# Three step buffers used in turn in a masked attention kernel: comparisons three units ahead, masks two

## The reference

```python
h = einsum('bnf,hfo->bhno', x, W)
s1 = einsum('bhno,ho->bhn', h, a1)
s2 = einsum('bhno,ho->bhn', h, a2)
e = leaky_relu(s1[..., :, None] + s2[..., None, :], negative_slope=0.2)
attn = softmax(where(adj > 0, e, NEG_INF), axis=-1)
h_prime = einsum('bhnm,bhmo->bhno', attn, h)
out = layernorm(x + transpose_and_reshape(h_prime), axis=-1)
```

## Time and profile before

| | |
|---|---|
| three runs, us | 2890.48, 2895.20, 2897.44 |
| the profiled execution | 2894.5 us, span 2892.8 us, mean granted TensorE clock 0.977 |
| one batch, start to start | 352 to 354 us; 32 units 284 to 287, the start of the next 66 to 69 |
| busy, share of the span | TensorE 92%, weight load 80%, VectorE 88%, ScalarE 81%, GpSimd 37% |
| ScalarE's comparisons (L603) | 3440, 2099.4 us busy |
| DMA | 390.20 MB, mean 135 GB/s |
| the chain that ended last | TensorE 33%, ScalarE 29%, VectorE 18%, issue 14%, DMA 3%, GpSimd 2% |

### The profile page before, as it was taken

The page is one execution under the profiler, slowest core; times in us unless marked ns, Lnnn a source line. Parts: engine busy times, 40 slices in busy tenths (PEclk is TensorE's granted clock), DMA queues, the critical chain, the costliest instruction groups (busy, mean ns, idle before and its releaser), DMA issues.

```text
span 2892.8 us, 126180 instructions
## 1 busy us (share of the span) xinstructions
PE 2666.2 (92%) x52546; PEld 2311.9 (80%) x52546; DVE 2532.7 (88%) x3881; ACT 2338.9 (81%) x3894; POOL 1083.5 (37%) x1011
## 2 busy tenths in 40 slices
PE   6999989999899998999989989899998999989996
PEld 3698867989579994898949988499884998759996
DVE  6898978999799997899888998889888998889996
ACT  4599965999569994799938998399983999839994
POOL 4633335333353324433253332533326333163331
PEclk9999999999999999999999999999999999999998
DMA  6467642675527754377543775447644476345763
GB/s 176 118 132 174 148 132 78 143 174 142 137 65 167 169 139 114 75 174 166 135 102 81 174 166 129 105 103 173 163 119 114 108 171 157 106 117 121 172 159 97
DMA packets 281205, 390.20 MB, mean 135 GB/s; under 512 B 161856, under 2 KB 161856, under 8 KB 280672
## 3 DMA queue, kind: packets, MB, share of 16 engines
q1 hardware_dynamic: 253536, 315.24, 40.7%
q0 software_dynamic: 27136, 67.12, 14.2%
HBM read 313.52 MB, written 34.14 MB: 120 GB/s over the span
## 4 chain that ended last, share of the span: by engine, by line
PE 33%; ACT 29%; DVE 18%; issue 14%; DMA 3%; POOL 2%; DVEq 1%; ACTq 0%; SPq 0%; POOLq 0%
ACT m_pos L603 26%; PE ps L526 12%; PE ps L497 6%; PE ps L557 6%; PE ps L558 5%; DVE m_neg L837 3%; DMA y<-in_x 3%; ACT adj_cut L569 2%; DVE m_pos L830 2%; DVE prod L801 2%; DVE prod_d L804 1%; DVE m_pos L816 1%; ACT xT L575 1%; PE ps L433 1%; DVE b_both L799 1%
## 5 line engine op out<-in xcount | busy, mean ns | idle before, releaser
L603 ACT ACTIVATE m_pos<-ps,s_steep 128x512 fp8e4<-128x512 f32 x3440 | 2099.4, 1087 | 371.3 <-PE ps L447 295.4
L526 PE MATMUL ps<-b_both,m_pos 128*128 128x130 f16 x16384 | 1018.8, 221 | 81.7 <-DVE total L666 63.0
L558 PE MATMUL ps<-d_lo,m_neg 128*128 128x65 f16 x16384 | 1034.7, 194 | 16.7 <-issue 16.4
L557 PE MATMUL ps<-d_hi,m_neg 128*128 128x65 f16 x16384 | 1034.9, 193 | 7.7 <-issue 7.6
L526 PEld LDWEIGHTS ps<-b_both,m_pos 128*128 128x128 fp8e5 x16384 | 965.7, 98 | 93.4 <-issue 91.4
L557 PEld LDWEIGHTS ps<-d_hi,m_neg 128*128 128x128 fp8e5 x16384 | 1016.0, 98 | 28.6 <-issue 28.5
L558 PEld LDWEIGHTS ps<-d_lo,m_neg 128*128 128x128 fp8e5 x16384 | 1006.7, 97 | 24.4 <-issue 10.3
L830 DVE TENSOR_TENSOR m_pos<-m_pos,maskT 128x1024 uint32<-128x1024 uint32 x512 | 630.4, 1249 | 165.6 <-ACT m_pos L603 153.3
L1000 POOL TENSOR_TENSOR den_scaled<-den_inv,bound 128x4 f32<-128x4 f32 x256 | 257.5, 1006 | 1269.1 <-DVE den_inv L677 1207.8
L837 DVE TENSOR_TENSOR m_neg<-m_pos,maskT 128x2048 uint32<-128x2048 uint32 x256 | 583.9, 2281 | 0.3
L497 PE MATMUL ps<-W_sb,xT 128*128 128x512 f32 x1024 | 461.4, 612 | 65.7 <-DVE prod_d L804 63.9
(11 more groups left out here) (95 smaller groups left out, 1578.5 us busy)
## 6 DMA issues: line engine op xcount, KB each, us to landing
adj_in<-in_adj SPq DMA_DIRECT2D x266, 512.0 KB, 4.7
s_bc<-s_rows SPq DMA_DIRECT2D x258, 256.0 KB, 3.6
x_in<-in_x SPq DMA_DIRECT2D x134, 256.0 KB, 4.2
x_sum<-in_x POOLq DMA_DIRECT2D x128, 256.0 KB, 4.9
y<-in_x POOLq DMA_DIRECT2D x32, 1024.0 KB, 9.9
out<-y SPq DMA_DIRECT2D x32, 1024.0 KB, 7.1
maskT<-adj_cut SPq DMA_TRANSPOSE x264, 3.6
m_neg<-in_x SPq DMA_DIRECT2D x10, 256.0 KB, 3.1
```

What stands on the lines that cost most here:

```text
L526: mm = pe.matmul(acc, mask, b_both[:, j, h, :, :], start=(j == 0 and it % 2 == 0), stop=(j == JC - 1 and it % 2 == 1))
L557: pe.matmul(acc, mask, d_hi[:, j, h, :], start=(j == 0), stop=False)
L558: mm = pe.matmul(acc, mask, d_lo[:, j, h, :], start=False, stop=(j == JC - 1))
L603: ins = nc.scalar.activation(chunk(m_pos[h % 2], j, 0, BLK), ps[:, BANK_S1 + h % 2, :], ACT.Relu, bias=s2_steep[:, j, h:h + 1], scale=STEE ...
```

## The change

There are three `m_pos` buffers instead of two, used in turn by the number of the unit in its batch. `before(unit)` gives how many units back the last user of the same buffer is (3; over the seam of two batches 2, 2 and 5 for units 0, 1 and 2).

- ScalarE's comparisons of unit u now wait for `neg_made` and `pos_summed` of u-3. Its program keeps the order; `copy_s1` moves from unit 30 behind the comparisons of unit 31.
- TensorE spreads the row of u+3 between the second and third tile of the negative sums of u, after a wait for ScalarE's comparisons of u+1; before, it spread u+2 between positive and negative sums. The row of unit 2 is spread at chunk 8 of the batch start.
- VectorE's iteration of u: `make_neg(u+1)`, maxima of x, `take_pos(u)`, scores, layer norm, two `make_pos` of u+2, comparisons of u+3, `take_neg(u)`. In the batch start the comparisons of unit 2 stand where `make_neg(1)` stood. In unit 31: `take_pos(31)`, masks of the next unit 0, `take_neg(31)`.
- `dve_slots` counts from u-3; the number of comparisons of each engine in a batch stays the same.
- SyncE loads the s1 row of u+3 instead of u+2.
- TensorE starts unit 0 when 7 chunks and a half are split, waits again before the second half and before its last three chunks, and turns the x tile of unit 0 behind the positive sums instead of ahead of them.

```diff
@@ -81,6 +81,6 @@
-        k, h = divmod((unit - 2) % UNITS, H)
-        if unit in (0, 1) or k * H + h == STAT_UNIT:
+        k, h = divmod((unit - 3) % UNITS, H)
+        if unit in (0, 1, 2) or k * H + h == STAT_UNIT:
             return DVE_SLOTS[1]
-        if (k and h in (2, 3)) or k * H + h in (0, STAT_UNIT + 1):
+        if k and h in (2, 3):
             return DVE_SLOTS[2]
@@ -88,2 +88,6 @@
+    def before(unit):
+        return {0: UNITS - (UNITS - 2), 1: UNITS + 1 - (UNITS - 1), 2: UNITS + 2 - (UNITS - 3)}.get(unit, 3)
     FIRST = 6
@@ -135,3 +139,3 @@
-        m_pos = [sb(f"m_pos{i}", [P, JC // 2, 2 * BLK], FP8) for i in range(2)]
+        m_pos = [sb(f"m_pos{i}", [P, JC // 2, 2 * BLK], FP8) for i in range(3)]
         m_neg = [sb(f"m_neg{i}", [P, JC // 2, 2 * BLK], FP8) for i in range(2)]
...
@@ -377,5 +381,10 @@
                                 store_block(g - 1, 1)
-                        if unit == UNITS - 2:
+                        if unit == UNITS - 3:
                             sp.wait_ge(s1_stored, 16 * KB * (b + 2))
-                        load_s1(u + 2, h % 2)
+                        if unit == UNITS - 1:
+                            sp.sem_inc(waited[sp.engine], 1)
+                            with sp.If(b < B - 1):
+                                load_s1(u + 3, (h + 1) % 2)
+                        elif unit:
+                            load_s1(u + 3, (h + 1) % 2)
                         for t in range(JC):
@@ -393,2 +402,6 @@
                                 load_x(JC * (b + 1) + t, t % 2, ((b + 1) * (JC // 2) + t // 2) % (NBLK * IT // 2))
+                        if unit == 0:
+                            with sp.If(b < 1):
+                                load_s1(2, 0)
+                            load_s1(u + 3, (h + 1) % 2)
                         if unit == STURN_UNIT + 1:
@@ -444,3 +457,7 @@
-            def spread_s1(unit):
+            def spread_s1(unit, u):
+                if type(u) is not int:
+                    pe.wait_ge(step_act, at(step_act, QUADS * (u - 1)))
+                    pe.sem_inc(waited[pe.engine], 1)
...
@@ -489,2 +506,4 @@
                         pe.wait_ge(s1_T_copied, b + 1)
+                    if jc == 8:
+                        spread_s1(2, b * UNITS + 2)
                     if jc == 1:
@@ -506,7 +525,6 @@
                         if unit == 0:
-                            pe.wait_ge(hi_d_made, b * JC + JC - 1)
-                            turn_x(JC * (b + 1), x_in[0][:], x_loaded[0], b * (JC // 2), 0)
                             pe.wait_ge(tiny_made, b + 1)
-                            pe.wait_ge(lo_made, at(lo_made, 2 * JC * (b + 1) - 2))
+                            pe.wait_ge(lo_made, at(lo_made, 2 * JC * b + JC - 1))
+                            pe.sem_inc(waited[pe.engine], 1)
                         pe.wait_ge(pos_read, at(pos_read, u))
@@ -517,2 +535,5 @@
                             pe.sem_inc(waited[pe.engine], 1)
+                            if unit == 0 and qd:
+                                pe.wait_ge(lo_made, at(lo_made, 2 * JC * (b + 1) - 7))
+                                pe.sem_inc(waited[pe.engine], 1)
                             for it in range(IT):
@@ -520,6 +541,6 @@
                                 for j in range(qd * JQ, (qd + 1) * JQ):
-                                    if unit == 0 and it == 0 and j == JC - 1:
-                                        pe.wait_ge(lo_made, at(lo_made, 2 * JC * (b + 1) - 1))
+                                    if unit == 0 and it == 0 and j >= JC - 3:
+                                        pe.wait_ge(lo_made, at(lo_made, 2 * JC * b + 2 * j + 1))
                                         pe.sem_inc(waited[pe.engine], 1)
-                                    mask = chunk(m_pos[hp], j, it * P, P).bitcast(FP8_WIDE)
+                                    mask = chunk(m_pos[unit % 3], j, it * P, P).bitcast(FP8_WIDE)
@@ -532,9 +553,5 @@
                             pe.wait_ge(lo_made, at(lo_made, 2 * JC * (b + 1)))
-                        if unit == UNITS - 2:
-                            pe.wait_ge(s1_T_copied, b + 2)
-                        spread_s1((unit + 2) % UNITS)
                         if unit == STAT_UNIT + 1:
                             turn_s1(b + 1)
-                        if unit and unit in TILE_UNIT:
+                        if unit in TILE_UNIT:
                             t = TILE_UNIT.index(unit)
@@ -553,2 +570,9 @@
                         for it in range(IT):
+                            if it == IT // 2 and unit < UNITS - 3:
+                                spread_s1(unit + 3, u + 3)
+                            if it == IT // 2 and unit >= UNITS - 2:
+                                if unit == UNITS - 2:
+                                    pe.wait_ge(s1_T_copied, b + 2)
+                                spread_s1(unit + 2 - UNITS, u + 2)
                             acc = ps[:, 2 + hp, it * O1:(it + 1) * O1]
@@ -590,3 +614,4 @@
-            def compare(u, h, unit):
+            def compare(u, unit):
+                h = unit % H
                 act.wait_ge(s1_spread, u + 1)
@@ -594,5 +619,5 @@
-                act.wait_ge(neg_made, at(neg_made, u - 1))
+                act.wait_ge(neg_made, at(neg_made, u - before(unit) + 1))
                 act.sem_inc(waited[act.engine], 1)
-                act.wait_ge(pos_summed, at(pos_summed, u - 1))
+                act.wait_ge(pos_summed, at(pos_summed, u - before(unit) + 1))
                 act.sem_inc(waited[act.engine], 1)
@@ -602,3 +627,3 @@
                             j = qd * JQ + c
-                            ins = nc.scalar.activation(chunk(m_pos[h % 2], j, 0, BLK), ps[:, BANK_S1 + h % 2, :], ACT.Relu,
+                            ins = nc.scalar.activation(chunk(m_pos[unit % 3], j, 0, BLK), ps[:, BANK_S1 + unit % 2, :], ACT.Relu,
                                                        bias=s2_steep[:, j, h:h + 1], scale=STEEP, saturate=False)
@@ -621,3 +646,3 @@
             act.wait_ge(s2_turned, 1)
-            compare(0, 0, 0)
+            compare(0, 0)
@@ -637,7 +662,6 @@
                             copy_scores(b + 1)
-                        if unit == STAT_UNIT + 2:
-                            copy_s1(b + 1)
                         if unit < UNITS - 1:
-                            compare(u + 1, (h + 1) % H, unit + 1)
+                            compare(u + 1, unit + 1)
                         else:
+                            copy_s1(b + 1)
                             exponentials(b + 1)
@@ -646,3 +670,3 @@
                                 act.sem_inc(waited[act.engine], 1)
-                                compare(u + 1, 0, 0)
+                                compare(u + 1, 0)
                         for i in late:
@@ -805,6 +829,8 @@
-            def compare(u, h, nth, unit):
+            def compare(u, unit, nth):
+                h = unit % H
                 hp = h % 2
-                dve.wait_ge(neg_made, at(neg_made, u - 1))
+                dve.wait_ge(neg_made, at(neg_made, u - before(unit) + 1))
                 dve.sem_inc(waited[dve.engine], 1)
@@ -815,3 +841,3 @@
                         j = qd * JQ + c
-                        ins = V.tensor_scalar(chunk(m_pos[hp], j, 0, BLK).bitcast(FP8_WIDE), s1_bc[hp][:], s2_neg[:, j, h:h + 1],
+                        ins = V.tensor_scalar(chunk(m_pos[unit % 3], j, 0, BLK).bitcast(FP8_WIDE), s1_bc[hp][:], s2_neg[:, j, h:h + 1],
                                               STEP_UP, ALU.is_gt, ALU.mult, saturate=False)
@@ -819,8 +845,8 @@
-            def make_pos(u, h, mask, qd, first_of_block=None):
-                hp = h % 2
+            def make_pos(u, unit, qd, blk):
+                mask = maskT[unit // H % 2]
                 if qd == 0:
-                    if first_of_block is not None:
+                    if unit % H == 0:
                         for slot in range(2):
-                            dve.wait_ge(piece_turned[slot], at(piece_turned[slot], 16 * IT * (first_of_block + 1)))
+                            dve.wait_ge(piece_turned[slot], at(piece_turned[slot], 16 * IT * (blk + 1)))
                             dve.sem_inc(waited[dve.engine], 1)
@@ -829,20 +855,12 @@
                 js = slice(qd * JQ // 2, (qd + 1) * JQ // 2)
-                V.tensor_tensor(words(m_pos[hp][:, js, :]), words(m_pos[hp][:, js, :]),
+                V.tensor_tensor(words(m_pos[unit % 3][:, js, :]), words(m_pos[unit % 3][:, js, :]),
                                 words(mask[:, js, :]), ALU.bitwise_and).then_inc(pos_made, 1)
-            def make_neg(u, h, mask):
-                hp = h % 2
+            def make_neg(u, unit):
+                mask = maskT[unit // H % 2]
                 dve.wait_ge(unit_done, at(unit_done, u - 1))
                 dve.wait_ge(pos_made, at(pos_made, QUADS * (u + 1)))
-                V.tensor_tensor(words(m_neg[hp][:]), words(m_pos[hp][:]), words(mask[:]), ALU.bitwise_xor
```

(47 more changed lines are left out.)

14 lines of the change are left out of this document (7 added, 7 removed).

## The result

| | before | after |
|---|---|---|
| median of 15 runs each, taken in turn | 2895.3 us | 2912.5 us |
| lowest to highest | 2890.2 to 2901.9 | 2902.3 to 2923.1 |
| profiled execution, its span | 2894.5, 2892.8 | 2903.2, 2901.4 |

The ratio is 1.0059, 95% interval 1.0045 to 1.0073: slower by 0.6%, where the prediction said 2874 us and faster. The profiled execution of after lies low among its own runs, which spread over 21 us; so the two profiles show 8.6 of the 17 us.

A forecast was written before the change was run, and what follows sets the result against it. ScalarE was taken as the slow engine in blocks two and three, TensorE as leading elsewhere. Lead and layer norm +13, batch end -16, batch start -24.5, unit 0 +6 sum to -21.5: 2874 us, range 2809 to 2897.

The forecast's parts named there:

- The likeliest case: Whole kernel: the forecast itself, faster at 2874 us, its own range 2852 to 2889; chance 0.55.
- rival B: Three blocks a batch: VectorE meets the layer norm 2.3 us sooner, the residual 1.1 later; +20, 2915 us; chance 0.12.
- Its own mark: Sign for rival B: waits of L526 above 100 us in all, in units 9 to 11 and 17 to 19.
- Part 1: Block two: ScalarE gains 6.1 us of lead, VectorE's new order eats 4.4, 1.7 are left; 2.0 us saved.
- Part 2: Third block: layer norm's wait for the residual starts unit 19 3.1 us later; blocks two and three +1.6 a batch, +13.
- Part 3: End of a batch: earlier maxima remove unit 31's 2.0 us delay in eight batches, -16.
- Parts 4 and 5: Batch start: 27.6 us become 24.1, -24.5 in seven starts; unit 0: +0.8 in eight batches, +6.
- The sign it gave: Batch start: the wait of L497 falls from 8.9 to some 5.4 us in each start.
- the clock was low too, so no gain there: Batch start: after 5.4 us of idle, TensorE's first matmul still takes 1.22 us, as before.
- `make_neg(1)` (2.2 us) leaving it gives nothing: Splitting: TensorE sets the pace (59.0 of 68.8 busy), so taking this mask out saves no time.
- Longer SyncE lead cost nothing: SyncE's row loads: rows are fetched as many iterations ahead of their reader as before, so no cost.
- the mark of 97%: Sign that the forecast is right: ScalarE still busy over 97% in blocks two and three.

The follow-up runs named there:

- Experiment 10: experiment 8's kernel with the residual's DMA also issued ahead of the x add; median 2821.0 us, ratio 0.9762 to the kernel before.
- experiment 9: experiment 8's kernel with ScalarE's comparisons held to two units' lead in units 3 to 27; median 2858.5 us, ratio 0.9885 to the kernel before.
- 15: Changed kernel with the negative mask of unit 1 moved back into the splitting, after chunk 10; median 2895.8 us, ratio 1.002 to the kernel before.
- experiment 11: experiment 6's kernel with unit 0 starting only after the remainders up to chunk 14, as before; median 2844.3 us, ratio 0.9837 to the kernel before.
- experiment 6: Changed kernel with layer norm one unit later and unit 2's s1 row fetched ahead of the cut pieces; median 2844.1 us, ratio 0.9826 to the kernel before.
- experiment 1: Changed kernel with unit 2's s1 row fetched ahead of unit 0's cut pieces in the first batch; median 2898.7 us, ratio 1.0023 to the kernel before.
- experiment 3: Changed kernel with VectorE's layer-norm steps, and GpSimd's power between them, one unit later; median 2853.5 us, ratio 0.9865 to the kernel before.
- experiment 8: experiment 6's kernel with VectorE's masks one unit ahead in units 1 to 27, two from there; median 2834.9 us, ratio 0.9804 to the kernel before.
- 5: Kernel before with VectorE's layer-norm steps, and GpSimd's power between them, one unit later; median 2866.7 us, ratio 0.9903 to the kernel before.
- 12: Kernel before with the residual issued ahead of the x add and layer norm one unit later; median 2862.2 us, ratio 0.9898 to the kernel before.
- 13: Experiment 10's kernel without GpSimd's 128 accumulating x add transfers; median 2826.0 us, ratio 0.9775 to the kernel before.

## Why the prediction was wrong, point by point

The parts on the end and the start of a batch came out in the main; those on the lead and on the layer norm, and one sentence on SyncE, outweighed them. The likeliest case had 0.55; what came is rival B, with 0.12. Its mechanism is the one that the experiments show, and its 2915 us is 2.5 from the median, but that closeness is partly luck. B had 55 us for the wait in two of three blocks; in the profiles blocks two and three cost 35.2. The rest of its sum was made up by what it did not have: 6.9 us at the first batch's start, 5.6 less gained at the other starts, and the median 9 us above the profiled execution, against 4.6 more gained at the end of a batch. Its own mark, waits for `take_pos` above 100 us, was not reached (84.0).

- **Part 1, the lead.** The lead at unit 8 grew as worked out: comparisons end 10.4 us ahead (4.6 before), 5.9 more against 6.1 worked out. What VectorE needs was put at 6.3 to 6.9; the floor measured is 6.7 to 7.5 (2.3 in the kernel before against my 1.9), as at unit 18 (timeline, ScalarE and TensorE; 1336.76 less 1330.08):

```profile
1322.45 7.63 ACT L628 ACTIVATE m_pos<-ps,s_steep 128x512 fp8e4<-128x512 f32 x13
...
1336.76 0.22 PE L547 MATMUL ps<-b_both,m_pos 128*128 128x130 f16 x1 [0.32 <-issue]
```

  Block two gained 0.3 us a batch, not 2.0. The reasoning that most of the lead is eaten was right; "1.7 are left" was too much. Experiment 10 shows why even a freed lead gives little: in second and third blocks TensorE has gaps of its own, 4.1 and 3.2 us a block, more than where something else is waited for (2.5 and 1.9 in experiment 9).
- **Part 2, the layer norm's wait.** This is the step that failed, and by size. Unit 19 was to start 3.1 us later after unit 8 than before; in the mean of eight batches it starts 5.3 later (104.9 us instead of 99.6). The terms, in means over the eight batches: the divide is 1.1 longer, right. `take_neg(15)` ends where it ended (74.3 us after unit 8), not 0.4 earlier. From landing to unit 19 it is 3.0 more (9.9 for 6.9), not 2.4. And the landing was put 19.4 us behind `take_neg(15)`, but came 20.7 behind it (22.4 in the fourth batch): the issue 0.3 later still, the transfer 0.9 longer (12.0 for 11.1). I took these two as constants from the one batch of the earlier trace rows; in the fourth batch they went from 4.31 to 6.05 and from 10.9 to 12.2. Of the 1.5 us that five units were to win back, 0.9 came. So blocks two and three cost 4.4 us a batch, not 1.6, and +35.2 in all, not +13.
- **Part 3, the end of a batch.** Right: 2.0 us predicted, no idle time before unit 31 in any batch; block four is 2.6 shorter.
- **Parts 4 and 5, start and unit 0.** From unit 31 to chunk 3: 24.1 predicted, 24.5 measured in the mean. The sign it gave, 5.4 us of wait there, was wrong (0.35): 3.8 us of idle time for nothing shown, ahead of chunk 0, and a slower first three chunks behind it (11.96 us for 24 matmuls instead of 10.56) stood in its place. That "the clock was low too, so no gain there" was wrong, to the good: the clock behind the start of chunk 3 was 1.00 instead of 0.59, worth 2.3 us a start. Of the two parts together -18.5 was predicted, and -12.9 came. The step that failed is that unit 0 costs only 0.8 more and that "`make_neg(1)` (2.2 us) leaving it gives nothing". At its new place the mask holds up GpSimd's last remainder by 2.0 us in each of eight batches, and from the end of unit 0's positive sums to unit 1 it takes 2.8 us more than before; with the mask back in the splitting (15) it takes 4.6 instead of 7.1, and in all 9.7 us came back. That unit 0's early start moves nothing holds (experiment 11 against 6: its positive sums end at the same time, to 0.2 us).
- **"Longer SyncE lead cost nothing"** failed: 6.9 us in the first batch, where the row of unit 2 was queued behind the cut pieces. I had counted iterations of lead, not what stands in SyncE's queue in front (experiment 1).
- The rest, 9 us between the profiled execution and the median, no profile shows. Runs of after lie within 21 us, of the kernel before within 12, of experiment 3 within 6, of experiment 6 within 8, so the wait for a DMA may bring the spread in; but the four runs of experiment 8, whose profile has no such wait in a third block, lie within 18. It stays open.

ScalarE was busy all of block two and 74 of 82.6 us in block three: the mark of 97% failed there. It worked on while VectorE stood, was done with unit 19's comparisons 17.5 us ahead of that unit, and then waited for TensorE's late transposes and row of s1 (4.0 and 1.9 us).

The Trainium skill, SBUF - State Buffer, "Who interferes with whom", gives the rule by which a VectorE instruction with two SBUF inputs holds up GpSimd's reads. The prediction used it for the divide, which in the whole run went from 1.0 to 1.96 us each, and did not for the last remainder, where the rows 1.13 and 3.10 show it again. In experiment 8, with masks one ahead in most units, the divide takes 1.0 us and the multiply behind it 1.29 instead of 0.61, so that the sum (2.29) is 0.28 shorter than in after (2.57).

## What to carry to other kernels

Ask of every engine with a fixed order what stands *behind* a wait for a DMA before moving work there: the wait does not need to be longer to cost more, and here the work that it blocked (masks for a later unit, then the read-out that frees TensorE's bank) was the change itself. Look at who issues the late transfer as well: in the changed kernel swapping two DMA issues on GpSimd was worth 63 us, more than the third buffer (22.6, experiment 6 against 5), though only 4.5 us where the reader comes late anyway (12 against 5). A lead is worth what its reader lets be spent, so look at where the far-ahead order is used (here the last four units; confining it to them gained 9 us at most). And take moved instructions past every engine that they now run beside.

## What the runs showed of the hardware

TensorE has gaps that wait for nothing the profile shows, up to 2.5 us long in experiment 10 and 3.0 in 8. In experiment 10 they are 60.4 us outside the splitting, in the fourth and fifth batch most of it in units 9, 10, 14, 17 and 22. They are smaller where something else is waited for: 35.9 us in experiment 9, with the same transfers as 8, which has 58.3. The kernel before had 31.2 of them on the same lines, beside 63 us of waits for `take_pos`. They also fell to 36.9 with 128 transfers of 256 KB fewer (13), in blocks where no other wait took their place; so the load of the DMA engines, or GpSimd's issuing, has a part in them. Experiment 10's page lists in its part on queues what the instructions come by:

```profile
q0 software_dynamic: 27136, 67.12, 14.5%
q8 instruction: 432, 7.08, 1.0%
```

(packets, MB, share of 16 engines.) That these packets come late behind data is the likeliest reading; no run here shows one packet's delay against one gap, so it stays open. The Trainium skill, Runtime: NRT & Kernel Launch, "Instruction fetch mechanics", says that the cost of fetching the next piece is mostly hidden. In this kernel, by that reading, some 2% of the time is not.

A divide of 128x4 numbers on GpSimd took 0.2 to 2.3 us, by what VectorE did beside it. And the accumulating transfer of 1 MB took 10.4 to 14.2 us from issue to landing in after's third blocks, against a median of 9.6 on the page and 9.9 to 12.0 in the same blocks before: a spread of 4 us within one execution, for which this kernel has to leave slack.
